# Attention with exact top-64 selection: where a branch flag is loaded and tested, and the extents of two small matrix products

## The reference

```
q, k = l2norm(heads of x @ Wq), l2norm(heads of x @ Wk)   # 16 heads of 64, 4 memory keys in front
dots = einsum('hg,bgij->bhij', W_pre_th, q @ k^T * 10)    # heads are mixed before the softmax
dots = where(key after query, -max, dots)
vk   = 64th largest value of each row of dots
dots = where(dots < vk, -max, dots)
attn = einsum('hg,bgij->bhij', W_post_th, softmax(dots))  # and mixed again behind it
out  = (attn @ v) * head_scale * sigmoid(gates) @ Wo
```

## Time and profile before

| | us |
|---|---|
| median of 3 runs | 3695.2 |
| lowest, highest | 3693.9, 3695.56 |
| the profiled execution | 3699.91 |
| its span, first to last instruction | 3697.8 |
| attention stage in it | about 893 to 3397 |

### The profile page before, as it was taken

How to read it: one execution, slowest core, us unless ns; L and a number is a source line. 1 busy time by engine, 2 the same in 40 slices (tenths; PEclk the granted TensorE clock), 3 DMA queues, 4 the chain that set the end, 5 groups by cost and what they waited for, 6 DMA issues and landing times. The chain is left out here.

```text
span 3697.8 us, 73987 instructions
## 1 busy us (share of the span) xinstructions
PE 3300.4 (89%) x22950; PEld 2111.1 (57%) x22950; DVE 2799.2 (76%) x6342; ACT 2575.1 (70%) x5953; POOL 2368.3 (64%) x6265
## 2 busy tenths in 40 slices
PE   7999999997788998888999898889988899988898
PEld 4445444443556656755656665555666555566466
DVE  6677776665688998678889867888886888886354
ACT  3444554443688989678889967888986888896321
POOL 2666766664777767677666768776677776675232
PEclk9999999997699999879999988999998999999899
DMA  3222222224456664346566435566534556641110
GB/s 119 97 86 103 103 91 86 89 82 149 132 167 175 183 180 114 86 140 173 167 173 170 103 102 149 172 179 174 149 89 127 160 169 173 185 106 35 54 35 29
DMA packets 363391, 467.04 MB, mean 126 GB/s; under 512 B 29460, under 2 KB 295060, under 8 KB 362520
## 3 DMA queue, kind: packets, MB, share of 16 engines
q1 hardware_dynamic: 362904, 461.54, 42.7%
HBM read 227.09 MB, written 234.36 MB: 125 GB/s over the span
## 5 line engine op out<-in xcount | busy, mean ns | idle before, releaser
L1099 ACT ACTIVATE junk<-D,nt 128x76 int8<-128x76 f32 (+62 forms) x1440 | 1070.2, 745 | 146.5 <-POOL nt L1187 112.4
L1004 PE MATMUL banks<-kr,E 128*128 128x128 f32 (+1 forms) x4672 | 704.5, 299 | 104.2 <-ACT AT L1122 78.9
L1004 PEld LDWEIGHTS banks<-kr,E 128*128 128x128 f32 (+1 forms) x4672 | 598.7, 201 | 226.5 <-issue 159.1
L977 PE MATMUL banks<-Sg,kpre 128*128 128x109 f32 (+51 forms) x1568 | 629.7, 500 | 25.2 <-POOL maskb L1253 13.4
L1122 ACT ACTIVATE AT<-banks 128x512 f32<-128x512 f32 (+3 forms) x768 | 344.7, 477 | 227.7 <-PE banks L1004 226.7
L1414 DVE SCALAR_TENSOR_TENSOR E<-D,vk,E 128x12 f32<-128x12 f32 (+56 forms) x512 | 383.1, 757 | 151.4 <-DVE vk L1370 92.3
L963 PE MATMUL banks<-kT,qT 64*128 64x343 f32 (+11 forms) x880 | 398.8, 536 | 96.4 <-DVE Sn L1326 89.0
L1326 DVE COPY Sn<-banks 128x686 f32<-128x686 f32 (+11 forms) x440 | 374.7, 852 | 142.8 <-PE banks L964 133.5
L1351 DVE SCALAR_TENSOR_TENSOR W<-SG,sgn,W 128x76 f32<-128x76 int8 (+14 forms) x480 | 421.4, 917 | 73.6 <-POOL W L1208 68.6
L585 DVE RECIPROCAL a_share<-a_share 128x512 f32<-128x512 f32 x128 | 419.9, 3323 | 69.2 <-POOL a_share L529 37.2
L1032 PE MATMUL banks<-AT,V 128*64 128x64 f32 x9216 | 396.9, 234 | 82.7 <-issue 74.7
(11 more groups left out here) (193 smaller groups left out, 5661.9 us busy)
## 6 DMA issues: line engine op xcount, KB each, us to landing
score_scratch<-Sn SPq DMA_DIRECT2D x96, 343.0 KB, 3.5
q_scratch<-a_share SPq DMA_DIRECT2D x32, 512.0 KB, 2.7
v_scratch<-a_share SPq DMA_DIRECT2D x32, 512.0 KB, 3.6
k_scratch<-a_share SPq DMA_DIRECT2D x32, 512.0 KB, 2.7
gate_scratch<-a_share SPq DMA_DIRECT2D x32, 512.0 KB, 2.8
kT<-k_scratch SPq DMA_DIRECT2D x32, 512.0 KB, 4.8
gateT<-gate_scratch SPq DMA_DIRECT2D x32, 512.0 KB, 10.0
qT<-q_scratch SPq DMA_DIRECT2D x31, 512.0 KB, 6.4
```

The lines of the kernel that those rows point to most:

```text
L977: out = nc.tensor.matmul(bank[:, 0:c], kpre[:].rearrange("p h r -> p (h r)"), Sg[:, g % 3, c0:c1], start=True, stop=not diagonal)
L1004: out = nc.tensor.matmul(ps[5 + i % 2][0:rows, c % 4 * P:(c % 4 + 1) * P], E[:, g % 4, c * P:c * P + rows], kr[:, g % 4, :], start=True, s ...
L1099: nc.scalar.activation(out, D[:, e, 1:1 + n], ACT.Sign, bias=nt[:, r, e:e + 1], scale=-1.0, accum_out=cnt[:, r, e:e + 1]).then_inc(s[f"cnt ...
```

## The change

Four things change. The tiles `onesb`, `deltab` and `maskb` get 128 rows, `onesb` also 128 columns; POOL clears `deltab` and `maskb` before it fills the first 8 rows, with two more MEMSETs in front of its wait for the constants. The product of `missed` now writes all 128 partitions of column 510, of which the first is read as before. On DVE the flag of pair k-3 is loaded directly behind `take(2k+1)`, and its branch stands behind the two `closest` of pair k-2 and ahead of `picked`; inside the branch, since `general` writes the buffer that `closest` reads, a wait for both `closest` is added. What pairs without a search do is not moved.

```diff
--- before.py
+++ after.py
@@ -843,9 +843,9 @@
         tie = sb("tie", [P, 4, 8])
         far = sb("far", [P, 8])
         bad = sb("bad", [P, 8], BF16)
-        onesb = sb("onesb", [P, 1], BF16)
-        deltab = sb("deltab", [R8, P], BF16)
-        maskb = sb("maskb", [R8, R8 + 1], BF16)
+        onesb = sb("onesb", [P, P], BF16)
+        deltab = sb("deltab", [P, P], BF16)
+        maskb = sb("maskb", [P, R8 + 1], BF16)
         flag = sb("flag", [1, 2], mybir.dt.int32)
         total = sb("total", [P, 8])
         rinv = sb("rinv", [P, 8])
@@ -987,8 +987,8 @@
             def missed(p, bank):
                 e = 2 * p % 8
                 pe.wait_ge(s["bad"], FP[p] + 1)
-                nc.tensor.matmul(bank[0:1, HELD:HELD + 1], onesb[:], bad[:, e:e + 1], start=True, stop=False)
-                return nc.tensor.matmul(bank[0:1, HELD:HELD + 1], onesb[:], bad[:, e + 1:e + 2], start=False,
+                nc.tensor.matmul(bank[:, HELD:HELD + 1], onesb[:], bad[:, e:e + 1], start=True, stop=False)
+                return nc.tensor.matmul(bank[:, HELD:HELD + 1], onesb[:], bad[:, e + 1:e + 2], start=False,
                                         stop=True)
 
             def post(g):
@@ -1248,9 +1248,11 @@
             nc.gpsimd.memset(zero[:], 0.0)
             nc.gpsimd.memset(Sg[:, :, HELD - R8:KW], 0.0).then_inc(s["konst"], 1)
             nc.gpsimd.memset(onesb[:], 1.0)
+            chain(nc.gpsimd.memset(deltab[:], 0.0))
+            chain(nc.gpsimd.memset(maskb[:], 0.0))
             pool.wait_ge(s["c_in"], 64)
-            nc.gpsimd.tensor_copy(deltab[:], delta[0:R8, :])
-            nc.gpsimd.tensor_copy(maskb[:], mask[:]).then_inc(s["small"], 1)
+            nc.gpsimd.tensor_copy(deltab[0:R8, :], delta[0:R8, :])
+            nc.gpsimd.tensor_copy(maskb[0:R8, :], mask[:]).then_inc(s["small"], 1)
             pool.wait_ge(s["sig"], 2)
             chain(ts(tab[:, K0:G3 + 1, :], tab[:, K0:G3 + 1, :], sigma[:, 0:1], None, ALU.mult))
             chain(tt(tab[:, K1, :], tab[:, G1, :], tab[:, XN, :], ALU.mult))
@@ -1405,6 +1407,8 @@
                     return
                 dve.wait_ge(s["vk"], FP[p] + 1)
                 with dve.If(found > 0):
+                    if searched(p + 1):
+                        dve.wait_ge(s["best"], 2 * FP[p + 1] + 2)
                     general(2 * p)
                     general(2 * p + 1)
 
@@ -1470,15 +1474,19 @@
                     dve.wait_ge(s["mixed"], MC[NT] + k - S + 1)
                     nc.vector.tensor_copy(flag[0:1, (k - 3) % 2:(k - 3) % 2 + 1],
                                           ps[2][0:1, HELD:HELD + 1]).then_inc(s["flag"], 1)
+                found = verdict(k - 3) if searched(k - 3) else None
                 scored(G, slots[1])
                 if searched(k - 2):
                     closest(2 * (k - 2))
                     closest(2 * (k - 2) + 1)
+                if searched(k - 3):
+                    threshold(k - 3, found)
+                if searched(k - 2):
                     picked(k - 2)
                 scored(G, slots[2])
                 if 0 <= k - 3 < S:
-                    found = verdict(k - 3) if searched(k - 3) else None
-                    threshold(k - 3, found)
+                    if not searched(k - 3):
+                        threshold(k - 3, None)
                     select(2 * (k - 3))
                 if k >= 10 and (k - 10) % 4 == 0 and (k - 10) // 4 < 2 * NB:
                     gated((k - 10) // 4)
```

## The result

The changed kernel takes 3656.41 us (median of 4 runs, 3648.66 to 3658.73), the kernel before on the same chip 3694.55 (3693.21 to 3695.56). The ratio is 0.9893, 95% interval 0.9876 to 0.9910: 38 us faster, where 88 were forecast. The profiled execution took 3658.73 us (span 3656.5). The time lies inside the stated range and the direction is right; the size is less than half of the forecast.

What follows compares the result with a forecast made beforehand. ACT bounds the last block, a chain through DVE and PE the others. DVE's 58 us plus PE's 30 make 88; 3699.9 less 88, less 4.7 for the profiled execution, gives 3607 us, range 3550 to 3672.

Steps and rivals of the forecast that it cites:

- What bounds the kernel: Attention stage: the last block goes by ACT, the others by a chain through DVE and PE; no engine above 89%.
- the 17 us that I took off for block 7: Last block: ACT leaves 2.25 us a sequence against some 6.6 of gaps, so 4.3 x 4 = 17 us come off.
- The gap ahead of `select`: DVE idle ahead of `select`: 151 us would fall to under 20; gross worth of the move 144 us.
- rival D: Sequencer does not run ahead past the logits, all 240 loads stand bare with 0.65 us: slower, 3725; chance 0.05.
- I take a third off: 58 us: DVE part: of 87 us left, a third turns into waiting for PE; 58 us won, ends 20 and 110.
- The bare load: Flag load behind the second tile's logits: uncovered 30 us in blocks 0 and 1, 10 us in blocks 2 and 3.
- The branch behind the searches: DVE, behind two MAX8 that hide it: zero cost from block 2 on, 0 to 0.2 us in blocks 0 and 1.
- The products: PE's mask and flag products at full extents: 1027 switches at 0.10 us go, net 88 us of PE.
- rival B: PE's switch gaps stay because the type changes (bf16 beside f32), DVE's 58 us stay: 3637 to 3645; chance 0.13.
- The flag's heavier loads: PE, flag product: loads of one column become 128 columns, costing 0.06 us for 240 pairs, 14 us.
- I took a third, 30: PE part: of net 88 us, a third reaches the end, 30 us; ends minus 10 and 60.
- The rival named A: ACT sets the pace beyond block 7: DVE part 20 us, half of PE's part, 15: 3660; chance 0.18.

Runs made afterwards that it cites:

- both edits of the last experiment: Changed kernel with the flag's load behind both searches of eight and POOL's wait for the selection ahead of `W` removed: 0.9771 of the kernel before, 84 us faster.

## Why the prediction was wrong

- **What bounds the kernel.** Block 7 gave 2.2 us where I said that ACT leaves 2.25, but that is luck: with 6 us less of exponentials it took as long (102.1 us), and with both edits of the last experiment 99.1, 3.4 us less than before (only there ACT has no idle time left). So the 17 us that I took off for block 7 rest on a bound that was not there. Over all blocks 111 us less of exponentials changed nothing either. Of the earlier trace rows I used the busy times and not the clock: block 1 ran at 0.57, and got 4.6 us shorter with the clock at 0.69.
- **The gap ahead of `select`.** It went, as said, to 3 us; the sequencer does run ahead, and rival D (no running ahead) is out. Its size, 144 us, was right and its weight was not.
- **The failed step is the weight: "I take a third off: 58 us".** All 144 us were worth 54 us, so nearly two thirds had to go. I had put the loss at waits for PE alone; the wait for `W` took more (46 against 28 and 12), and I had left that line (73.6 us) out of my rows.
- **The bare load.** Forecast 40 us of idle, measured 43, in part by luck: I counted 60 pairs with a search in blocks 0 and 1, and there are 48, at 0.3 to 0.5 us 14 to 24 us and not 30, while in block 2 of the second sequence 3.1 us stayed bare for 8 pairs, 0.39 for each and not 0.15. But I took it off one for one ahead of the third, so that it counted 27 us, and its place makes it count 31. The net of move and bare load is 52 - 31 = 21 us with full products, as measured directly (0.9949 against 0.9893), and 8 by the move alone, against 58. I had even named what is queued behind it, copies that PE waits for, and gave that no price.
- **The branch behind the searches.** Zero, as said: the load and it together hide under two MAX8.
- **The products.** The gaps of 0.10 us went where I had counted them, so rival B is out: between f32 and bf16 of the same extents the next product starts 0.03 us behind. PE's busy time fell by 83 us (forecast 88; 84 with the products alone, 6 with the move alone). The flag's heavier loads (of `onesb`, which are the weights, and not `bad`) cost no 0.06 us: the products start 0.03 us apart as before. The end got 19 us of it, where I took a third, 30.
- **The rival named A** had the right time (3660), by the wrong cause as far as the runs show: it has ACT set the pace.

## What to carry to other kernels

Idle time on an engine that is one of several in a ring need not be worth its length, and here its worth seems to depend on where in the round it stands: price it by a run that leaves the stalled instructions out, before moving them. A register load and a branch are best put behind two or more long instructions that are already free to start, and not ahead of anything that another engine waits for. A small product with other extents than its neighbours cost a gap of 0.10 us on either side here, and padding it with zeros cost nothing that shows: the mask product takes 0.17 us in place of 0.18, and its weight load 0.11 in place of 0.09, beside running products.

## What the runs showed that I had not expected

Moving transfers of 0.5 MB earlier, out of a wait of 4 us, made the changed kernel 0.7% slower and the one before 0.85%, and the wait that grew depended on the round: for stores of scores with round 4, for loads of scores with round 6. And a wait that no longer guards anything after a reordering (POOL's for the selection) was worth 31 us in the changed kernel, nearly as much as the change, though it let two instructions of different engines overlap and slow each other.
